# Query-key-value product on four column tiles, value transposes and projection one step later, query copy on ScalarE

## What is computed

```python
h = modulate(rmsnorm(x, norm1_w), sh_msa, sc_msa)
qkv = (h @ qkv_w.T).reshape(B, N, 3, H, D)
q, k = rope(rmsnorm(q)), rope(rmsnorm(k))
attn = softmax(einsum('bnhd,bmhd->bhnm', q, k) * D ** -0.5)
o = einsum('bhnm,bmhd->bnhd', attn, v).reshape(B, N, C)
x = x + g_msa * (o @ proj_w.T + proj_b)
h2 = modulate(rmsnorm(x, norm2_w), sh_mlp, sc_mlp)      # the tail: feed-forward
x = x + g_mlp * (silu(h2 @ w1.T) * (h2 @ w3.T) @ w2.T)
```

## Time and profile before

| | us |
|---|---|
| three runs | 209.03, 207.35, 207.10, median 207.35 |
| the profiled execution, whole time | 207.43 |
| its span in the profile | 205.4 |
| PE, DVE, ACT, POOL busy | 180.9, 166.1, 129.4, 141.3 |
| granted PE clock | 1.00 all the way, as the page's slices show |
| attention steps | 29.2 to about 126, with feed-forward from 120 |
| feed-forward alone | about 136 to 158 |

### The profile page before, as it was taken

How to read it: one execution, slowest core, us unless ns; L and a number is a source line. 1 busy time by engine, 2 the same in 40 slices (tenths; PEclk the granted TensorE clock), 3 DMA queues, 4 the chain that set the end, 5 groups by cost and what they waited for, 6 DMA issues and landing times.

```text
span 205.4 us, 6100 instructions
## 1 busy us (share of the span) xinstructions
PE 180.9 (88%) x2039; PEld 142.3 (69%) x2039; DVE 166.1 (81%) x498; ACT 129.4 (63%) x377; POOL 141.3 (69%) x333
## 2 busy tenths in 40 slices
PE   2598887997999999799999998899998899999963
PEld 2345565786687777677676777799997677888642
DVE  6699898896989999997776534668889799999882
ACT  1367798776867777576546763454442468999741
POOL 8889798998989797958810682434542847668651
PEclk9999999999999999999999999999999999999999
DMA  5955006800000000000000000000000000010111
GB/s 93 289 137 207 0 10 254 359 6 0 3 3 2 5 5 0 3 0 5 3 3 0 5 0 3 0 0 5 2 0 2 0 3 0 0 30 28 51 51 51
DMA packets 10428, 8.30 MB, mean 40 GB/s; under 512 B 3106, under 2 KB 9887, under 8 KB 9887
## 3 DMA queue, kind: packets, MB, share of 16 engines
q1 hardware_dynamic: 7006, 7.25, 10.3%
q10 hardware_dynamic: 3392, 0.68, 1.7%
HBM read 6.86 MB, written 1.07 MB: 39 GB/s over the span
## 4 chain that ended last, share of the span: by engine, by line
PE 40%; DVE 17%; issue 8%; POOL 5%; ACT 4%; POOLq 0%; ACTq 0%; DVEq 0%
PE bank L1895 5%; DVE qkpad L1604 5%; PE bank L875 5%; PE bank L1886 5%; PE bank L863 5%; PE bank L864 4%; PE bank L1975 4%; ACT probs L1302 2%; PE bank L908 2%; POOL rstd L515 2%; PE bank L1907 1%; PE bank L1920 1%; PE bank L992 1%; PE bank L1949 1%; PE bank L972 1%
## 5 line engine op out<-in xcount | busy, mean ns | idle before, releaser
L1604 DVE TENSOR_REDUCE qkpad<-bank 128x4 f32<-128x512 f32 x64 | 41.0, 684 | 10.1 <-PE bank L1886 9.2
L1302 ACT ACTIVATE probs<-bank 128x512 f32<-128x512 f32 x64 | 34.7, 594 | 22.6 <-PE bank L1895 22.5
L1895 PE MATMUL bank<-qTm,kBD 32*128 32x128 f32 x512 | 37.1, 283 | 0.1
L1886 PE MATMUL bank<-kBD,qTs 32*128 32x256 f32 x224 | 32.0, 399 | 4.4 <-DVE qkpad L1604 3.4
L1895 PEld LDWEIGHTS bank<-qTm,kBD 32*128 32x128 f32 x512 | 31.0, 186 | 0.9 <-issue 0.6
L1886 PEld LDWEIGHTS bank<-kBD,qTs 32*128 32x128 f32 x224 | 19.7, 184 | 10.3 <-DVE qkpad L1604 6.3
L575 ACT ACTIVATE th<-bank 128x256 f32<-128x256 f32 x24 | 9.2, 384 | 19.4 <-PE bank L864 16.0
L1975 PE MATMUL bank<-probs,vpad 128*32 128x128 f32 x512 | 18.6, 277 | 2.0 <-ACT probs L1302 2.0
L1975 PEld LDWEIGHTS bank<-probs,vpad 128*32 128x32 f32 x512 | 12.6, 109 | 8.4 <-ACT probs L1302 7.3
L1130 POOL TENSOR_TENSOR partner<-qk,rope 128x96 f32<-128x96 f32 x32 | 14.4, 471 | 2.0 <-ACT qk L1344 2.0
L1949 PE MATMUL bank<-qkvT,hT 128*128 128x384 f32 x32 | 15.3, 571 | 0.5 <-ACT hT L1319 0.5
(11 more groups left out here) (253 smaller groups left out, 521.4 us busy)
## 6 DMA issues: line engine op xcount, KB each, us to landing
gate<-in_cond_dram SPq DMA_DIRECT2D x1, 1024.0 KB, 4.7
x<-gate_rows SPq DMA_DIRECT2D x1, 1024.0 KB, 4.3
y<-gate_rows SPq DMA_DIRECT2D x1, 1024.0 KB, 6.4
res<-gate_rows SPq DMA_DIRECT2D x1, 1024.0 KB, 9.8
out_dram<-res SPq DMA_DIRECT2D x7, 128.0 KB, 1.8
xin<-in_x_dram ACTq DMA_DIRECT2D x2, 256.0 KB, 5.4
xin<-in_x_dram SPq DMA_DIRECT2D x1, 512.0 KB, 5.7
ada_n<-in_L_cond_ada_w_dram SPq DMA_DIRECT2D x1, 256.0 KB, 6.2
```

The source lines that it names most:

```text
L1302: q.activation(probs[2 * r + i][:, :, :, :].rearrange("p f a t -> p (f a t)"), bank[E_BANK[i]][:, :], ACT.Exp, scale=SCALE).then_inc(s_p, 1)
L1604: q.tensor_reduce(out_, score_bank(b, r, i)[:, :].rearrange("p (f a t) -> p f a t", f=2, a=2), X_AXIS, ALU.max, negate=True).then_inc(s_ma ...
L1886: last = q.matmul(bank[S_BANK[i]][:, f * 2 * T:(f + 1) * 2 * T], qTs[b % 2][rows, f, :], kBD[b % NKB][rows, f, :, :].rearrange("p a t -> p ...
L1895: last = q.matmul(bank[E_BANK[i]][:, (2 * f + k) * T:(2 * f + k + 1) * T], kBD[t % NKB][rows, f, k, :], qTm[t % 2][rows, f, :], start=True ...
```

## The change

The product L1949 is issued, for sequences 6 to 15, as four products of 32 columns each, on the four column tiles. The PE transpose of the attended values moves from between L1949 and L1975 of the next step to the head of the full-size block one step later still, and with it, one step later, the projection, DVE's gated projection and residual sum, and ACT's squares of x1; oT becomes two buffers, and LAST_A goes from B + 2 to B + 3. In the full-size block the transposes of queries and keys (t + 3) and of the input (t + 6) come first, then projection, token_major and the queries with maxima. ACT copies oT between its first two exponentials, copies the modulated input before the queries with maxima, and takes the masked query copy qTs (from sequence 3 on) from DVE; for that it waits for DVE's kBD (new semaphore s_kb). DVE does kBD first after the row maxima.

```diff
-LAST_A, LAST_POOL = B + 2, B + 1
+LAST_A, LAST_POOL = B + 3, B + 1
...
-        oT = sb("oT", [128, T])
+        oT = many("oT", 2, T)
...
+            def queries(b):
+
+                if not is_seq(b):
+                    return
+                a.wait_ge(s_kb, b - MASKED_BY_ACT + 1)
+                q.activation(qTs[b % 2][:, :, :].rearrange("p f t -> p (f t)"), bank[T_BANK][:, 0:2 * T], ACT.Identity,
+                             scale=rowmask[:, 0:1]).then_inc(s_kq, 1)
...
                 a.wait_ge(s_oTp, b + 1)
-                wait(a, s_proj, b)
-                q.activation(oT[:, :], bank[P_BANK][:, 256:384], ACT.Copy).then_inc(s_oT, 1)
+                wait(a, s_proj, b - 1)
+                q.activation(oT[b % 2][:, :], bank[P_BANK][:, 256:384], ACT.Copy).then_inc(s_oT, 1)
...
                 exp(t, 0, 1)
+                attended(t - 2)
                 exp(t, 0, 0)
...
+                modulated_input(t + 6)
                 queries_and_max(t + 1)
-                modulated_input(t + 6)
+                queries(t + 3)
                 exp(t, 1, 0)
                 exp(t, 1, 1)
-                if t < B:
-                    attended(t - 1)
...
-                spread_of(t - 2)
+                spread_of(t - 3)
...
+                if b >= MASKED_BY_ACT:
+                    made.then_inc(s_kb, 1)
...
                 rowmax(t + 2, 0, 1)
+                keys_apart(t + 3)
                 reciprocals(t - 1)
-                gated_projection(t - 2)
                 attended(t - 1)
-                keys_apart(t + 3)
-                queries(t + 3)
+                gated_projection(t - 3)
...
-                after_attention(t - 2)
+                after_attention(t - 3)
...
-                q.matmul(front_bank(b)[:, 128:512], hT[b % 2][:, :], qkvT[:, :], start=True, stop=True).then_inc(s_qkv, 1)
+                if b < FRONT_B:
+                    q.matmul(front_bank(b)[:, 128:512], hT[b % 2][:, :], qkvT[:, :], start=True, stop=True).then_inc(s_qkv, 1)
+                else:
+                    for c in range(4):
+                        last = q.matmul(front_bank(b)[32 * c:32 * c + 32, 128:512], hT[b % 2][:, 32 * c:32 * c + 32], qkvT[:, :],
+                                        start=True, stop=True)
+                    last.then_inc(s_qkv, 1)
...
                 round_(t, 0)
-                projection(t - 2)
+                attended(t - 2)
+                queries_and_keys(t + 3)
+                input_turned(t + 6)
+                projection(t - 3)
                 token_major(t - 1)
...
                 queries_and_max(t + 1)
-                queries_and_keys(t + 3)
-                input_turned(t + 6)
...
                 queries_keys_values(t + 6)
-                if t < B:
-                    attended(t - 1)
                 weighted_values(t, 0)
```

More of the change, by code:

```diff
@@ L68 @@
 FRONT_B = 6
+MASKED_BY_ACT = 3
 TBL = 4 * DH
-LAST_A, LAST_POOL = B + 2, B + 1
+LAST_A, LAST_POOL = B + 3, B + 1
 C_UNITS = U + UNIT - 1
@@ L318, in dit_then_linear_attention @@
         s_kq = sem("s_kq")
+        s_kb = sem("s_kb")
         warmed = sem("warmed")
@@ L1465, in _ @@
                     b_rest(t - B)
-                if t >= B:
-                    attended(t - 1)
                 summed(t)
                 values(t + 6)
-                spread_of(t - 2)
+                spread_of(t - 3)
                 if t == B - 6:
@@ L1473, in _ @@
                     q.activation(outw[:, :], outw_n[:, :], ACT.Copy, scale=0.5).then_inc(pv_a, 1)
-            blocks_scalar(a, 2)
+            blocks_scalar(a, LAST_A - B)
         @block.vector
@@ L1632, in keys_apart @@
                 wait(v, s_e1, ROUNDS * (b - NKB + 1))
-                q.tensor_tensor(kBD[b % NKB][:, :, :, :],
-                                bank[T_BANK][:, 2 * T:4 * T].rearrange("p (f t) -> p f t", f=2).unsqueeze(2).to_broadcast([128, 2, 2, T]),
-                                pmask[:, :].unsqueeze(1).unsqueeze(3).to_broadcast([128, 2, 2, T]), ALU.mult)
+                made = q.tensor_tensor(kBD[b % NKB][:, :, :, :],
+                                       bank[T_BANK][:, 2 * T:4 * T].rearrange("p (f t) -> p f t", f=2).unsqueeze(2).to_broadcast([128, 2, 2, T]),
+                                       pmask[:, :].unsqueeze(1).unsqueeze(3).to_broadcast([128, 2, 2, T]), ALU.mult)
+                if b >= MASKED_BY_ACT:
+                    made.then_inc(s_kb, 1)
             def queries(b):
@@ L1648, in gated_projection @@
                 v.wait_ge(s_proj, b + 1)
-                v.wait_ge(s_oq, min(b + 2, B))
+                v.wait_ge(s_oq, min(b + 3, B))
                 wait(v, s_x1, b)
@@ L1767, in _ @@
                     centred()
-            blocks_vector(v, 2)
+            blocks_vector(v, LAST_A - B)
         @block.tensor
@@ L1904, in projection @@
                 e.wait_ge(s_oT, b + 1)
-                e.wait_ge(s_oT4, min(b + 2, B))
+                e.wait_ge(s_oT4, min(b + 3, B))
                 wait(e, s_x1g, b)
-                q.matmul(bank[O_BANK][:, 0:D], oT[:, :], projT[:, :], start=True, stop=True).then_inc(s_proj, 1)
+                q.matmul(bank[O_BANK][:, 0:D], oT[b % 2][:, :], projT[:, :], start=True, stop=True).then_inc(s_proj, 1)
             def token_major(b):
@@ L1966, in weighted_values @@
                     wait(e, s_on, b)
-                    wait(e, s_x1g, b - 1)
+                    wait(e, s_x1g, b - 2)
                     if b == 0:
@@ L1984, in attended @@
                 wait(e, s_qTm, min(b + 3, B))
+                wait(e, s_oT, b)
                 q.transpose(bank[P_BANK][:, 256:384], o[:, :, :].rearrange("p h d -> p (h d)"), ident[:, :]).then_inc(s_oTp, 1)
@@ L2052, in _ @@
                     b_rest(t - B, t % 2)
-                    attended(t - 1)
-            blocks_tensor(e, 2)
+            blocks_tensor(e, LAST_A - B)
 _INS = ['x', 'cond_1024', 'fside_BxSx3_0', 'L0_cond_norm1_w', 'L0_cond_qkv_w', 'L0_cond_q_norm_w', 'L0_cond_k_norm_w',
```

## The result

The changed kernel takes **208.43 us** (median of 20 runs, 208.17 to 209.49), the kernel before 207.39 (20 runs): a ratio of 1.0046, 95% interval 1.0031 to 1.0060. That is a small loss, 1.0 us, inside the 1% called no change, 0.4 under the 208.8 forecast and inside its range. The profiled execution took 208.6 us with a span of 206.9. That execution holds a stretch before the loop, 20 to 25 us, with a mean granted clock of 0.68, so more than half of it at the lower level (1.2 GHz), behind 5 us in which PE was busy for 3.9. The trace of before has 1.00 in 20 to 25 us.

The account below looks back on a forecast made before the run. PE was taken to bound ordinary steps, with the exponentials' chain close behind, and DVE the late ones; 0.1 - 0.5 + 0.8 + 0.35 + 0.7 = +1.45 on 207.43 gave 208.9, as median 208.8 us, range 204.4 to 211.2.

Parts of the forecast that it names:

- R1 to R0 goes by the exponentials: Score round 1 to next round 0: exponentials need 2.99, so of PE's 0.28 saved only 0.07 arrives.
- R0 to R1: Score round 0 to round 1: the transpose of o adds a pass, 0.11, so 2.56 becomes 2.67, PE last.
- The long stretch of 3.38 behind them is unchanged: Late steps on DVE: from round 1's maxima to the next round 0's stays 3.38, as before.
- step of the first kind: Loop step in which PE never idles: 5.62 becomes 2.67 + 2.99 = 5.66, three times, +0.1 in all.
- Late DVE steps: Steps 6, 8, 9 and 10, where DVE's maxima come late: without qTs on DVE -0.12 each, -0.5 in all.
- Keys first: PE's block, steps 3 and 1: work queued behind the wait for POOL's keys comes later, together +0.8.
- The rival that these terms are not paid: POOL's step 3 and the tail find cover for the added terms: 206.8 us, chance 0.10.
- Behind step 10: Steps 11 to 15, without the product: the moved transpose adds 0.11 each, less 0.20 in step 15, +0.35.
- The tail: After the loop: oT's wait goes, -0.53, but POOL's xs2 comes late for PE, +1.25; together +0.7.
- DVE as the bound: Rival, whole loop: DVE was the real bound and the exponentials move up with it; 203.9 us, chance 0.21.
- ACT's queue through qTs: Rival, ACT ahead of round 1's exponentials: qTs holds them by 0.25 in 13 steps, +3.2, 212.0 us; chance 0.17.
- the serial tiles: Rival, product on four column tiles: they don't run side by side, 0.6 too long in ten steps, 215 us; chance 0.04.

Follow-up runs that it names:

- e_dveq: The changed kernel with the masked query copy qTs back on DVE behind kBD: 209.29 us, ratio 1.0085 to the kernel before.
- e_notiles: The changed kernel with the query-key-value product as one full product again, no column tiles: 208.50 us, ratio 1.0048 to the kernel before.
- e_key3: The changed kernel with the transposes of queries and keys behind token_major in step 3 alone: 208.19 us, ratio 1.0041 to the kernel before.
- e_attlast: The changed kernel with the transpose of o last in PE's block and its copy behind ACT's second exponentials: 207.69 us, ratio 1.0026 to before.
- e_rootlast: The changed kernel with POOL's last root mean square (unit 7) behind the normed input of unit 5: 207.11 us, ratio 0.9990 to before.
- e_b_qact: The kernel before with qTs on ACT, kBD first on DVE and normalised o ahead of the gated projection: 207.07 us, ratio 0.9988.
- e_before_rootlast: The kernel before with POOL's last root mean square (unit 7) behind the normed input of unit 5: 207.13 us, ratio 0.9995.
- e_best: The changed kernel with o's transpose last (steps 10 to 15: between round 1 and weighted values) and POOL's last root behind unit 5's normed input: 209.79 us, 1.0105.

## Why the prediction was right, and where it was not

The total lay 0.4 from the forecast, and that closeness is luck: two stages of the table were wrong by -1.5 and +1.25 and cancel. The chain of exponentials and the tail were right by their mechanism.

- **R1 to R0 goes by the exponentials.** Right: 2.96 to 2.99 in all steps with a product, with tiles or without. The product on tiles 0.67, as worked out. Of PE's 0.28 only 0.1 arrived.
- **R0 to R1.** 2.72 for 2.67. PE is not last: the exponentials with oT between them are, by 0.08.
- **What bounds the even steps** is the step that failed. I took them as DVE's, with a fixed stretch of 3.38 behind the maxima of round 1, and read POOL (69% busy on the page) only where PE waited for it. "The long stretch of 3.38 behind them is unchanged" was wrong: its sum x shrank from 0.83 to 0.66, as it started later into POOL's rot, and the next maxima start 1.50 after rot in both kernels. I also counted steps 6, 8, 9 and 10 as late; the waits for the maxima stand in steps 4, 6, 8 and 9. The 5.66 for a step of the first kind (5.69 measured) was right by its chain, but that even steps take 5.69 as well was not foreseen: they lie on the floor that POOL and DVE set.
- **Late DVE steps**, -0.5 forecast. Of the -1.1 in R0(0) to R0(10), 0.75 is step 9, where the style operations replace the seeds. Kernel before, then the change, DVE:

```profile
83.03 0.39 DVE L1567 SCALAR_TENSOR_TENSOR csilu<-ctanh,condT 128x16 f32<-128x16 f32 x1
83.46 0.65 DVE L1568 TENSOR_SCALAR csilu<-csilu 128x16 f32<-128x16 f32 x1
```
```profile
82.78 0.17 DVE L1575 SCALAR_TENSOR_TENSOR csilu<-ctanh,condT 128x16 f32<-128x16 f32 x1
82.98 0.17 DVE L1576 TENSOR_SCALAR csilu<-csilu 128x16 f32<-128x16 f32 x1
```

  In e_dveq they are 0.39 and 0.65 again. From the maxima of round 1 to the next ones is 4.17 before, 3.53 in e_notiles and 3.96 in e_dveq: 0.64 of the gain is a shorter stretch, and 0.2 is the lateness through qTs that I had costed at 0.12. That the stretch shrinks by a shift against POOL's operations is read from the rows and not tested by itself.
- **Keys first**, +0.8 forecast. Step 3 does lose (R0 to R1 4.16, before 3.83), but step 4 gives 0.30 of it back (2.72, before 3.02), as the wait of 0.44 for DVE falls away there; e_key3 shows the same the other way. I had added a local delay to the sum without asking who would have waited anyway. The rival that these terms are not paid held for this one.
- **Behind step 10**, +0.35 forecast, +1.6 measured. I counted the transpose's pass and not the wait that came with it: queries and maxima behind oT of the same step. e_attlast gives back 1.2. It is the largest mis-sized term upwards, and its error cancels that of the first ten steps (+0.4 forecast, -1.1 measured).
- **The tail**, +0.7 forecast, +0.5 measured, by the mechanism named: oT's wait of 0.53 gone, a new one of 1.11 (1.25) for POOL's xs. e_rootlast and its control show it.
- **The rivals.** DVE as the bound fell with e_b_qact, ACT's queue through qTs with the exponentials 1.26 after R1 (ACT is last from R0 to R1, but through oT and by 0.05 a step), the serial tiles with the 0.67. By the Trainium skill (TensorE: Matmul & The Clock Gate, What overlaps and what doesn't) column tiles would have exposed their loads; the 0.67 for eight of them disagrees.

Left open: that POOL and DVE set the floor is read from thirteen versions that all come to 11.3 to 11.4 us in steps 6 and 7, whatever PE, ACT or DVE was relieved of, and from what e_key3 and e_attlast gave back. A version with less work on POOL was not tried, so the cause is argued from the rows and not shown by an experiment, and in the change itself, where the exponentials' chain is level with it, less work on POOL alone would gain nothing by this reading.

## What to carry to other kernels

Measure the period of each engine's own recurring instruction before deciding what bounds a pipelined loop: an engine with few idle rows there and the same period in every version is likely its floor, whatever its busy share over the whole page. Then look in each step at what ends last, as a second chain can be level with it. A local delay or saving counts only if no such floor takes it back. When an operation moves by a step, look for the next reader of its result in each queue, at the edge of the loop (the tail's due times) and at the single buffers (o) above all; that is where the losses of this change (+1.6 and +0.5) were.

## What was unexpected of the hardware

- DVE's sum of two SBUF tiles takes 0.27 to 0.28 alone and up to 0.85 beside POOL's rot (0.83 in the kernel before, 0.85 in e_key3), ending 0.14 to 0.15 after it where it is held; csilu, 128x16, takes 0.17 or 0.65. The Trainium skill (SBUF — State Buffer, SBUF: two separate sides) says that the two engines share a pair of ports under an exclusive lock, held for a whole instruction by the one that starts first, and that a DVE operation takes part with two SBUF inputs (against a POOL operation that reads SBUF) or in a two-port mode. The sum, with its two SBUF inputs, agrees: it starts 0.05 behind rot (64.66 and 64.61) and ends behind it; the wait of csilu's second operation, which has one, agrees only if it runs in such a mode, which no row tells.
- Five of fourteen profiled executions held a stretch at a lower granted clock, in different places: 0.68 for 20 to 25 us in the change's, 0.74 from 200 us to the end in e_before_rootlast's, where the whole execution has a span of 206.2 against 205.0 to 205.1 at 1.00. It came in some executions of each kernel and not in others of the same one; only e_best had it in five of six.
